# Dense layers of a graph network: four half buffers for counted edges, fetches behind them, block 0 turned in mid-sum, own product first, X added by GpSimd

## What is computed

```python
x = _layernorm(x + _L0_gnn_ref(x, ...))           # edge convolution
x = _layernorm(x + _L1_gnn_ref(x, ...))           # attention: out = LN(sum/weights + x)*gamma + beta
x = _layernorm(x + _L2_gnn_ref(x, src, dst, ...)) # mean over neighbours:
    h = x @ W_self.T + (segment_sum(x[src], dst) / deg) @ W_neigh.T + bias
    h = LN(h) * gamma + beta
x = _layernorm(x + _L3_gnn_ref(x, ...))           # two gated relational layers:
    msg_r = (sigmoid(x_j @ gate_w[r])[:, None] * x_j) @ w[r]        # r = 0, 1 by edge type
    out = segment_sum(msg, row) + x @ root + bias                   # relu between the two
```

## Time and profile before

| what | value |
|---|---|
| median of 3 runs | 1936.45 us (1935.54 to 1938.03) |
| span of the profiled execution | 1934.6 us |
| TensorE busy | 1608.4 us (83%) |
| VectorE busy | 1167.7 us (60%) |
| GpSimd busy | 705.2 us (36%) |
| ScalarE busy | 471.2 us (24%) |
| mean granted TensorE clock | 0.929 |
| dense layers begin at | 1357.5 us |

### The profile page before, as it was taken

How to read it: one execution, slowest core, us unless ns; L and a number is a source line. 1 busy time by engine, 2 the same in 40 slices (tenths; PEclk the granted TensorE clock), 3 DMA queues, 4 the chain that set the end, 5 groups by cost and what they waited for, 6 DMA issues and landing times. The chain is left out here.

```text
span 1934.6 us, 27686 instructions
## 1 busy us (share of the span) xinstructions
PE 1608.4 (83%) x7565; PEld 981.3 (51%) x7566; DVE 1167.7 (60%) x2310; ACT 471.2 (24%) x884; POOL 705.2 (36%) x605
## 2 busy tenths in 40 slices
PE   6755956776498999998888459998498899999998
PEld 6751633335443555554555435554246545874486
DVE  5779958884365777775467766665774832113222
ACT  4301103432212555554344210000110111001100
POOL 0001877887094776660000347775330010000000
PEclk9997988998698999999899569999799999999999
DMA  0017844005802766682388337776104201430033
GB/s 25 0 47 285 275 136 120 1 1 172 306 27 92 210 197 187 187 169 45 126 317 331 101 100 211 210 209 171 27 1 144 96 1 72 155 122 1 0 136 135
DMA packets 76346, 248.96 MB, mean 129 GB/s; under 512 B 14901, under 2 KB 28582, under 8 KB 68346
## 3 DMA queue, kind: packets, MB, share of 16 engines
q1 hardware_dynamic: 38618, 147.08, 21.1%
q0 software_dynamic: 34592, 96.87, 18.9%
q10 hardware_dynamic: 3072, 4.20, 0.7%
HBM read 215.93 MB, written 32.00 MB: 128 GB/s over the span
## 5 line engine op out<-in xcount | busy, mean ns | idle before, releaser
L664 POOL DMA_INDIRECT tab_slots<-slot_words,slot_address x160 | 238.1, 1488 | 244.5 <-issue 233.3
L693 POOL DMA_INDIRECT e_rows<-tab_h,idx_h x176 | 178.6, 1015 | 293.4 <-POOLq L50 219.8
L1443 PE MATMUL dense_pY<-weights,dense_xT_block 128*128 128x512 f32 x640 | 284.3, 602 | 0.0
L1491 PE MATMUL dense_pY<-parts,dense_number 128*128 128x512 f32 x1000 | 237.7, 399 | 7.1 <-DMA dense_number<-tab_edges_to 7.1
L994 POOL DMA_INDIRECT e_rows<-tab_q,idx_q x192 | 182.0, 948 | 99.4 <-issue 38.9
L1491 PEld LDWEIGHTS dense_pY<-parts,dense_number 128*128 128x128 f32 x1000 | 188.7, 189 | 54.8 <-DMA dense_number<-tab_edges_to 8.6
L787 PE MATMUL e_pS<-e_rows,e_onehot_ring 128*128 128x512 f32 x352 | 194.2, 643 | 22.1 <-DVE e_rows L763 19.2
L1443 PEld LDWEIGHTS dense_pY<-weights,dense_xT_block 128*128 128x128 f32 x640 | 121.9, 194 | 143.1 <-issue 143.1
L1067 PE MATMUL e_pS<-e_rows,e_onehot_f 128*128 128x512 f32 x384 | 181.4, 596 | 0.0
L877 PE MATMUL count_pA<-count_onehot_d,count_onehot_s 128*128 128x512 f16 (+1 forms) x576 | 117.4, 352 | 63.8 <-DVE count_onehot_d L855 60.3
L763 DVE TENSOR_TENSOR e_rows<-e_rows,e_pW 128x1024 f32<-128x1024 f32 x88 | 107.3, 1220 | 69.3 <-DMA e_rows<-tab_h,idx_h 69.0
(11 more groups left out here) (312 smaller groups left out, 2448.4 us busy)
## 6 DMA issues: line engine op xcount, KB each, us to landing
basis_piece<-in_L_gnn_basis_pieces SPq DMA_DIRECT2D x32, 2048.0 KB, 7.9
dense_number<-tab_edges_from SPq DMA_DIRECT2D x20, 1280.0 KB, 5.4
tab_edges_from<-counts_turned SPq DMA_DIRECT2D x10, 1280.0 KB
tab_edges_to<-counts_total SPq DMA_DIRECT2D x10, 640.0 KB
dense_number<-tab_edges_to SPq DMA_DIRECT2D x10, 640.0 KB, 4.6
tab_w<-basis_wout ACTq DMA_DIRECT2D x128, 32.0 KB
weights<-tab_w SPq DMA_DIRECT2D x4, 1024.0 KB, 6.3
weights<-in_L_gnn_W_T SPq DMA_DIRECT2D x3, 1024.0 KB
```

Of the source, the lines that this page charges most:

```text
L664: pool.indirect_dma_start(self.table, bass.IndirectOffsetOnAxis(self.address[:, t:t + 1], 0), self.words[:, t, :], None).then_inc(self.pla ...
L693: pool.indirect_dma_start(self.rows[:, q, s, :], None, self.table, bass.IndirectOffsetOnAxis(self.idx[:, j * 2 + s:j * 2 + s + 1], 0)).the ...
L1443: ins = self.nc.tensor.matmul(self.banks.at(g), self.xt[:, b % 2, c, :], weights[:, c, :], start=c == 0, stop=c == 3)
L1491: ins = self.nc.tensor.matmul(self.banks.at(self.first + b), self.number[:, b % 2, r * NB + k, :], self.parts[r][n][:, k, :], start=k == 0 ...
```

## The change

- **Buffers.** `dense_number` is seen as four half slots in `sum2` (REL / relations times two) and as two whole slots in the others. `sum2`'s loads 0 to 3 wait for nothing; the five fetches come after them, and loads 4 to 9 after the fetches. Each stage has its own `loaded` semaphores. In the later sums load 0 goes to the second slot.
- **Order of products.** The own product is first in each block. Block b + 1 is turned after block b's own product, so that block 0's first product no longer stands behind turn 1.
- **Block 0 in mid-sum.** The next projection's block 0 is turned ahead of sum 5 instead of sum 9, and ScalarE's copy of it stands ahead of round 4 of the roots instead of round 9.
- **Own product of `proj2`.** ScalarE copies it to `held` ahead of the high part; VectorE only counts the bank as emptied; GpSimd adds the bias later, after the block's high part.
- **X added by GpSimd.** Scale, add X and add beta stand together on GpSimd for each block; VectorE waits for X-added.

```diff
 class Projection:
-    def multiply(self, pe, b):
-        pe.wait_ge(self.copied, self.base + b + 1)
-        for w, weights in enumerate([s[0] for s in self.split] + [self.own[0]]):
...
+    def multiply(self, pe, b, w):
+        if w == 0:
+            pe.wait_ge(self.copied, self.base + b + 1)
+        weights = self.split[w - 1][0] if w else self.own[0]
+        self.banks.wait_free(pe, self.bank(b, w))
...
     def high(self, act, b):
         act.wait_ge(self.multiplied, self.base + b + 1)
+        if self.own[1] is None:
+            self.nc.scalar.copy(self.own[2](b), self.banks.at(self.bank(b, 0)))
...
     def low(self, v, b):
         v.wait_ge(self.high_out, self.base + b + 1)
+        if self.own[1] is None:
+            wait(v, self.banks.emptied, self.bank(b, 0))
+            v.sem_inc(self.banks.emptied, 1)
+        else:
+            nc.vector.tensor_tensor(self.own[2](b), self.banks.at(self.bank(b, 0)), self.own[1](b), ALU.add
+                                    ).then_inc(self.banks.emptied, 1)
...
 class Aggregation:
+        self.slots = 2 * REL // relations
+        self.number = number.rearrange("p q (h k) n -> p (q h) k n", k=relations * NB)
+    def slot(self, b):
+        return (b + (self.base > 0)) % self.slots
     def load(self, sp, b):
-        wait(sp, self.summed, self.base + b - 1)
+        if self.base and b < 2:
+            before = 2 if self.base == NB else 1
+            wait(sp, self.summed, self.base - (1 - b) * before)
+        else:
+            wait(sp, self.summed, self.base + b - self.slots + 1)
...
         def _(sp):
             for b in range(NB):
-                sum2.load(sp, b)
-                if b == 1:
+                if b == sum2.slots:
                     sp.wait_ge(multiplied, NB)
                     for tile, source in fetches[0]:
                         sp.dma_start(tile, source).then_inc(fetched, 16)
+                sum2.load(sp, b)
...
         def _(pool):
+            for b in range(NB):
+                ah = acc[:, b, :].rearrange("p (h d) -> p h d", h=H)
+                nc.gpsimd.tensor_tensor(ah, ah, inverse[:, b, :].unsqueeze(2).to_broadcast([P, H, DH]), ALU.mult
+                                        ).then_inc(scaled, 1)
+                pool.wait_ge(scaled, b + 1)
+                nc.gpsimd.tensor_tensor(acc[:, b, :], acc[:, b, :], X[:, b, :], ALU.add).then_inc(x_added, 1)
+                pool.wait_ge(x_added, b + 1)
+                nc.gpsimd.tensor_tensor(X[:, b, :], X[:, b, :], V["L1_gnn_ln_beta"], ALU.add).then_inc(shifted, 1)
             for b in range(NB):
                 pool.wait_ge(turned, b + 1)
-                nc.gpsimd.tensor_tensor(X[:, b, :], X[:, b, :], V["L2_gnn_beta"], ALU.add).then_inc(aside_done, 1)
+                nc.gpsimd.tensor_tensor(X[:, b, :], X[:, b, :], V["L2_gnn_beta"], ALU.add)
+                pool.wait_ge(high_out, b + 1)
+                nc.gpsimd.tensor_tensor(held[:, b, :], held[:, b, :], V["L2_gnn_bias"], ALU.add).then_inc(aside_done, 1)
...
             def project_all(proj, ready, fetches):
+                if not fetches:
+                    pe.wait_ge(*ready(0))
+                    proj.turn(pe, 0)
+                wait(pe, fetched, FETCH * fetches)
                 for b in range(NB):
+                    for w in range(proj.nw):
+                        proj.multiply(pe, b, w)
+                        if w == 0 and b + 1 < NB:
+                            pe.wait_ge(*ready(b + 1))
+                            proj.turn(pe, b + 1)
...
-                    if b == NB - 1 and following:
+                    if b == NB // 2 and following:
...
-                if n == NB - 1:
+                if n == NB // 2 - 1:
                     proj3.copy(act, 0)
...
-                    v.wait_ge(scaled, n + 1)
-                    link(nc.vector.tensor_tensor(acc[:, n, :], acc[:, n, :], X[:, n, :], ALU.add))
-                    v.sem_inc(x_added, 1)
+                    v.wait_ge(x_added, n + 1)
                     norm1.stats(link, n, 0, acc[:, n, :])
```

More of the change, by code:

```diff
@@ L1435, in copy, with bank @@
         self.nc.scalar.copy(self.xt[:, b % 2, :, :], self.pt[:, :, :]).then_inc(self.copied, 1)
-    def multiply(self, pe, b):
-        pe.wait_ge(self.copied, self.base + b + 1)
-        for w, weights in enumerate([s[0] for s in self.split] + [self.own[0]]):
[L1440 to L1445, removed]
+    def bank(self, b, w):
+        return self.first + b * self.nw + w
+    def multiply(self, pe, b, w):
[3 more added lines that the diff above has]
+        self.banks.wait_free(pe, self.bank(b, w))
+        for c in range(4):
+            ins = self.nc.tensor.matmul(self.banks.at(self.bank(b, w)), self.xt[:, b % 2, c, :], weights[:, c, :],
+                                        start=c == 0, stop=c == 3)
+        if w == self.nw - 1:
+            ins.then_inc(self.multiplied, 1)
     def scale(self, b, gate):
@@ L1451, in high @@
         act.wait_ge(self.multiplied, self.base + b + 1)
+        if self.own[1] is None:
+            self.nc.scalar.copy(self.own[2](b), self.banks.at(self.bank(b, 0)))
         for w, (_, high, _, gate) in enumerate(self.split):
-            ins = self.nc.scalar.activation(high[:, b, :], self.banks.at(self.first + b * self.nw + w), ACT.Copy,
+            ins = self.nc.scalar.activation(high[:, b, :], self.banks.at(self.bank(b, w + 1)), ACT.Copy,
                                             scale=self.scale(b, gate))
@@ L1457, in low @@
     def low(self, v, b):
-        nc, g = self.nc, self.first + b * self.nw
+        nc = self.nc
         v.wait_ge(self.high_out, self.base + b + 1)
+        if self.own[1] is None:
[4 more added lines that the diff above has]
+                                    ).then_inc(self.banks.emptied, 1)
         for w, (_, high, low, gate) in enumerate(self.split):
-            nc.vector.scalar_tensor_tensor(low[:, b, :], self.banks.at(g + w), self.scale(b, gate),
+            nc.vector.scalar_tensor_tensor(low[:, b, :], self.banks.at(self.bank(b, w + 1)), self.scale(b, gate),
                                            high[:, b, :].bitcast(F32), ALU.mult, ALU.subtract
                                            ).then_inc(self.banks.emptied, 1)
-        nc.vector.tensor_tensor(self.own[2](b), self.banks.at(g + self.nw - 1), self.own[1](b), ALU.add
-                                ).then_inc(self.banks.emptied, 1)
 class Aggregation:
     def __init__(self, nc, stage, relations, banks, number, sems, count_rows, parts):
-        self.nc, self.base, self.relations, self.banks, self.number = nc, stage * NB, relations, banks, number
+        self.nc, self.base, self.relations, self.banks = nc, stage * NB, relations, banks
         self.loaded, self.summed = sems
@@ L1475, in __init__ @@
         self.first = banks.reserve(NB)
+        self.slots = 2 * REL // relations
+        self.number = number.rearrange("p q (h k) n -> p (q h) k n", k=relations * NB)
+    def slot(self, b):
+        return (b + (self.base > 0)) % self.slots
     def load(self, sp, b):
[L1478 to L1480 removed]
+        if self.base and b < 2:
[3 more added lines that the diff above has]
+            wait(sp, self.summed, self.base + b - self.slots + 1)
+        sp.dma_start(self.number[:, self.slot(b), :, :].bitcast(F32), self.count_rows(b)
+                     ).then_inc(self.loaded[self.slot(b)], 16)
     def sum(self, pe, b, source):
[L1483 to L1484 removed]
+        pe.wait_ge(self.loaded[self.slot(b)], (b // self.slots + 1) * 16)
         self.banks.wait_free(pe, self.first + b)
@@ L1490, in sum @@
                 for n in range(2):
-                    ins = self.nc.tensor.matmul(self.banks.at(self.first + b), self.number[:, b % 2, r * NB + k, :],
+                    ins = self.nc.tensor.matmul(self.banks.at(self.first + b), self.number[:, self.slot(b), r * NB + k, :],
                                                 self.parts[r][n][:, k, :], start=k == 0 and r == 0 and n == 0,
@@ L1517, in dense_layers @@
         gates_summed, gated, high_out = sem("gates_summed"), sem("gated"), sem("high_out")
-        loaded, summed = [sem(f"loaded{k}") for k in range(2)], sem("summed")
+        loaded = [[sem(f"loaded{stage}_{k}") for k in range(2 * REL if stage == 0 else 2)] for stage in range(3)]
+        summed = sem("summed")
         fetched, stored = sem("fetched"), sem("stored")
@@ L1526, in aggregate @@
         def aggregate(stage, relations, rows):
-            return Aggregation(nc, stage, relations, banks, number, (loaded, summed), rows, parts)
+            return Aggregation(nc, stage, relations, banks, number[:, :, :, :], (loaded[stage], summed), rows, parts)
         of_X, of_held = (lambda b: X[:, b, :]), (lambda b: held[:, b, :])
@@ L1531, in dense_layers @@
         from_block = lambda b: edges_from[b * P:(b + 1) * P, :].rearrange("p (k n) -> p k n", n=P)
-        proj2 = project(0, of_X, [(W[0], *parts[0], None)], (W[1], lambda b: V["L2_gnn_bias"], of_held))
```

(1 more changed line is left out.)

17 lines of the change are left out of this document (removed).

## The result

The median went from 1937.24 us (four runs, the three shown and one more) to 1920.26 us: 17.0 us less. The ratio, estimated from all runs, is 0.9908 with a 95% interval of 0.9895 to 0.9921; the two medians alone give 0.9912, which lies inside it. Forecast were 1919.9 us and a gain of 16.6.

The account below looks back on a forecast made before the run. TensorE was taken to bound the dense layers, with gaps only in the first projection, first sum and joint. Gains 7.3 + 9.3 = 16.6 us; 1934.6 - 16.6 = 1918.0, with 1.85 constant 1919.9 us; range 1914.5 to 1929.

Parts of the forecast that it names:

- First projection: First dense stage: fewer TensorE pauses, so it ends at 1454.6 against 1461.94; 7.3 us gained.
- The run-in: Before the first projection: block 0 normalised 2.7 us later, yet first product at 1379.1 against 1381.53 before.
- The loss of clock: First projection after the initial wait: slow clock costs TensorE 1.8 us.
- lateness grows to about 1.1 us: First projection: VectorE delivers blocks every 7.85 us, TensorE wants them every 7.31, until some 1410 us.
- rival B: First projection: VectorE's three operations each wait a whole 1.27 us GpSimd instruction, block about 8.3 us; 1931 us, chance 0.15.
- E: First projection: VectorE, blocked at three operations per block, bounds all ten blocks; kernel slower, 1946 us, chance 0.04.
- operations on two SBUF operands: First projection: GpSimd stretches VectorE's L1384, L1385 and L1389, to 1.797, 1.637 and 1.387 us; statistics and low part not.
- That is what removes the pauses.: First projection: the chain from product to next normalised block, 6 to 9 us, gets 10.7 us instead of 7.31.
- Sum and joint: First sum to second projection: no load waits, block 1 starts at S + 64.6, S being the sum's start; 9.3 us gained.
- the 2.9 us in hand: First sum: fifth load lands about S + 15.8, TensorE needs it at S + 18.7, S being the sum's start.
- What follows: Later stretches without gaps: reordered products, turns and loads leave TensorE's work the same; costed at nothing.

Follow-up runs that it names:

- two turns: Changed kernel with block 1 of the next projection also turned in mid-sum, its copy ahead of round 6 of the roots; 1914.10 us, 0.9880 of the kernel before.
- both improvements: Changed kernel with block 1 also turned in mid-sum and X added by VectorE again; 1909.29 us, 0.9858 of the kernel before.

## Why the prediction was right

It was right in the total and in the mechanism of both terms. That the total came within half a microsecond is luck: the first term was 1.3 us too small and the second 1.0 too large.

*First projection, 7.3 forecast, 8.6 measured* (104.46 to 95.83). The run-in came as worked forward: first product 21.6 us after D forecast, 21.74 measured, so the 2.9 us that GpSimd's three operations in a row cost were seen ahead. The loss of clock was 5.47 - 3.60 = 1.87, forecast 1.8. The ten blocks with their turns took 72.2 us, not 72.6. Wrong was the step "lateness grows to about 1.1 us". There was none. I had taken the most crowded block of the earlier trace rows, 7.25 us, for every block. VectorE's rows over the projection after show the mean instead:

```profile
L1385 DVE SCALAR_TENSOR_TENSOR acc<-acc,dense_norm_rstd,x 128x512 f32<-128x512 f32 x8 | 11.3, 1416 | 0.3
...
L1384 DVE SCALAR_TENSOR_TENSOR acc<-acc,dense_norm_mv,vectors 128x512 f32<-128x512 f32 x8 | 8.0, 999 | 0.3
L1389 DVE TENSOR_SCALAR x<-acc,dense_norm_mv,dense_norm_rstd 128x512 f32<-128x512 f32 x9 | 7.9, 876 | 0.3
```

That is 3.29 us for the three, where the crowded block has 1.797 + 1.637 + 1.387 = 4.82 and an undisturbed one 2.05. In the kernel before the mean over its first projection was 3.15 (1.494, 1.004 and 0.651), so the change stretched VectorE by 0.14 us a block in the mean and relieved it of two adds of 0.68.

A single collision looks like this in the profile after:

```profile
1375.29 1.26 POOL L1597 TENSOR_TENSOR acc<-acc,x 128x512 f32<-128x512 f32 x1
1375.34 1.75 DVE L1384 SCALAR_TENSOR_TENSOR acc<-acc,dense_norm_mv,vectors 128x512 f32<-128x512 f32 x1
1376.62 1.59 POOL L1599 TENSOR_TENSOR x<-x,vectors 128x512 f32<-128x512 f32 x1
1377.13 1.63 DVE L1385 SCALAR_TENSOR_TENSOR acc<-acc,dense_norm_rstd,x 128x512 f32<-128x512 f32 x1
```

GpSimd's add ends at 1376.55 and VectorE's L1384 0.54 us later; the next two end at 1378.21 and 1378.76. In this profile every stretched L1384 and L1385 of the first projection ends 0.54 to 0.56 us after the end of a GpSimd instruction, and every stretched L1389 0.28 or 0.29 after one; with ten more GpSimd operations it is the same within 0.01. So VectorE's instruction waits out the GpSimd instruction beside it and then finishes, and "meet only at semaphores" in the first section is too simple: these two engines also meet here. The Trainium skill says (SBUF — State Buffer, section "Who interferes with whom") that one engine is blocked until the other's instruction ends; these rows agree. What rival B needed besides is that each of the three waits a whole GpSimd instruction of 1.27 us, 3.8 a block. It was 3.29 - 2.05 = 1.24 a block in the mean, as 8 of the 30 did not collide and others came when part of GpSimd's instruction was done; so B fell, and E for the same reason. The reading "operations on two SBUF operands" was not quite right: L1389 is stretched too and has one 128x512 input beside two columns.

*"That is what removes the pauses."* I gave that to the order of turns alone. It is enough alone, but the runs show a second cure: with the order undone one pause of 1.02 us came back, with the add of X undone none, with both undone all three.

*Sum and joint, 9.3 forecast, 8.3 measured* (171.11 to 162.84 from the first to the second sum). No wait for a load, as said. With two slots again the load in the same place of the queue, issued 5.26 us after the sum's start in both, let TensorE go on at 16.1; the changed kernel comes to it at about 19, so the 2.9 us in hand were there. The sum took 47.51 with the turn, forecast 47.1; block 1 began 64.45 us after the sum's start, forecast 64.6; the pause was 6.04 us for the copy at L1435, forecast 6.6. Two sizes in the joint were off. The clock cost 6.17 - 3.60 = 2.57 us after the pause instead of 1.8. And one turn was miscounted: before, block 1's start at 1537.68 had turn 2 behind it; now turn 2 comes after block 1's own product, 0.44 us more.

*What follows, costed at nothing:* 301.5 us from the second sum to the end in both.

What the forecast didn't ask is which edit pays. The buffers are worth 7.1 to 7.4 us, the turn behind the own product 6.6 at the start of the sum, and the turn in mid-sum 1.7 without a second one. The add of X on GpSimd costs 2.9 us of run-in, of which 1.1 reached the end in one pair of profiles and 3.2 in the other. These don't add up to 16.9, since the order of turns and the add of X stand in for each other: both undone, the first sum starts 8.8 us later, which is the whole gain of the first projection. The own product on ScalarE and its bias on GpSimd were never undone by themselves; what they are worth beside the other edits is not shown.

## What to carry to other kernels

When two edits cure the same pause, undo each alone and both together; here one of them cost 2.9 us of run-in and bought nothing that the other hadn't. A gain in one stage reaches the end only as far as the slowest chain beside it: list what is queued ahead of the next needed instruction on each in-order engine (here a 0.57 us copy behind twenty roots), and move that instruction too. Price a shared resource by its mean over the stretch as well as by its worst block, and let the two be the bounds.

## What was not expected of the hardware

The loss of clock after one and the same pause differs from run to run. After the run-in, whose code is the same in these four, the first eight matmuls of the first product took 5.14 us (two slots), 5.47 (changed kernel), 5.69 (two turns) and 6.71 (block 0 turned late); in the two with X on VectorE and the turn behind the own product, whose run-in is alike too, 6.67 and 5.39 (both improvements). At full clock they take 3.60, so 1.5 to 3.1 us were lost at the lower of the two levels, 1.2 instead of 2.4 GHz (granted clock 0.50 from 1521.67 to 1524.00 us in the changed kernel). At the joint the same eight matmuls took 5.21 to 6.78 us after pauses of 4.6 to 7.7, and 6.17, 6.37 and 6.78 after pauses that agree within 0.01 us (6.03 and 6.04). In these runs a forecast of a pause's price could not be closer than that; the best cure at the joint was to have almost no pause, as in the kernel with two turns.
